# Cross-attention in a decoder kernel: the queries' product ahead of the turn, turned keys beside the turned queries, and two of four masked query copies on ScalarE

## The chip, the core and the metric

The kernel runs on one core of a Trainium2 chip. Its time is device microseconds from the launch's first to its last work; lower is better. TensorE multiplies and transposes into PSUM (eight banks of 128 partitions x 512 f32), VectorE and ScalarE read PSUM and SBUF, GpSimd reads SBUF only. Engines run their instructions in program order and wait for one another on semaphores.

## What is computed

Two decoder layers over 16 samples of 128 tokens with 256 channels. The change lies in the second of six sublayers, the cross-attention of layer 0 (32 heads of 8 channels, queries and keys normalised for each head).

```python
x = x + _L0_attn_ref(_layernorm(x), ...)
x = x + _L0_xattn_ref(_layernorm(x), ctx_2048, L0_xattn_Wq, L0_xattn_Wk, L0_xattn_Wv)   # this one
x = x + _L0_ffn_ref(_layernorm(x), L0_ffn_weight)          # a linear layer with quantised input
x = x + _L1_attn_ref(_layernorm(x), ...)                    # linear attention, then two more
...
def _L0_xattn_ref(x, context, Wq, Wk, Wv):
    q = x @ Wq.T                       # k_raw, v_raw likewise from context, 32 heads of 8
    ...
    q = _rmsnorm(q)                    # over the 8 channels of a head
    k = _rmsnorm(k)
    scores = jnp.einsum('bhnd,bhmd->bhnm', q, k) * scale
    attn = jax.nn.softmax(scores, axis=-1)
    out = jnp.einsum('bhnm,bhmd->bhnd', attn, v)
```

## The kernel before, in words

Each sublayer is a `Part`: on every engine a function `step(s)` issues what is due in step s, for several samples at different stages. In the part "cross-attention and quantised linear" (function `cross_attention_and_quantised_linear`, tensors `xa.*` and `ql.*`) step s handles sample s (its products), b = s-1 (its turn and scores), a = s-2 (weighted values), c = s-3 and d = s-4 (the quantised linear layer), and the layer norms of the samples s+1 and s+2. The steps 6 to 13 are a hardware loop, the others are written out. The order on each engine is the order of the code in `step`; the first steps are interleaved with the last of the channel attention (`ca.*`, through `s.meet()`), the last with the first of the linear attention (`la.*`).

One sample goes through these stages (lines of the kernel before):

- TensorE: the keys' product (L851) and the queries' product (L870), both into PSUM bank 6. ScalarE squares them (L782, `xa.sq`) and copies them to SBUF (L785, tensor `raw` inside `g.spare`). VectorE sums the squares of each head and makes a first guess of the inverse root (L705, L707, L176). GpSimd refines it in ten small instructions (L181 to L199, `xa.norm`).
- VectorE multiplies by it (L685, `xa.qkn`). TensorE transposes the result, "the turn": queries into the first half of bank 5 (`turn2`, L863), keys into bank 4 (`turn`, L865).
- ScalarE copies the turned keys to SBUF (L777, `xa.kT`), VectorE the turned queries four times over, each copy multiplied by another column of the constant `g.quad`, which masks one of four heads in each group of 32 rows (L698, `xa.qT`, 128 x 1024).
- TensorE: scores in two halves of 16 heads (L841 twice) into banks 0 to 3; ScalarE: exponentials of each half (L765). The second half of the scores waits for the exponentials of the first. Weighted values of sample a go to bank 4 (L894), are copied (L797, `xa.oT`), turned into all of bank 5 (L919) and divided (L739, L743); GpSimd adds them to x (L652). The values' product is L924, the turn of the next layer norm L931.
- In between VectorE makes the statistics of the two layer norms (L323 to L327, for `xa.stats` and `ql.stats`), GpSimd their inverse roots (L640, L634), VectorE applies them (L332), and the quantised linear layer takes L721 to L747 on VectorE, L649 on GpSimd, L792 on ScalarE and L881 and L914 on TensorE.

Of the kernel before, what the change touches and what calls it, by code (L numbers as in the profile page):

```python
# [16 lines left out]
ALU = mybir.AluOpType  # L17
ACT = mybir.ActivationFunctionType
AX = mybir.AxisListType

P = 128
# [32 lines left out]
def upto(at, back=0, per=1, more=0):  # L54

    assert at.base is not None or (at.n + 1 - back) * per + more > 0
    return (at.i + (1 - back)) * per + more
# [503 lines left out]
def cross_attention_and_quantised_linear(nc, g, ctx, room):  # L561
# [93 lines left out]
    def vector(dve):  # L655
# [17 lines left out]
        def step(s):  # L673
# [18 lines left out]
            if s.base is None and s.n == 1:  # L692
                s.meet()
            if b.on:
                dve.wait_ge(qk_turned, upto(b))
                if b.past(2):
                    dve.wait_ge(scores_done, upto(b, back=2, per=2))
                nc.vector.tensor_tensor(qT[:, b.par, :, :, :], spread(turn2[:, 0, :, :], 2, 4),  # L698
                                        spread(spread(g.quad[:], 1, C), 3, P), ALU.mult).then_inc(qT_ready, 1)
            if c.on:  # L700
                dve.wait_ge(x_added, upto(c))
                layer_norm_stats(nc, n, g.x[:, c.i, :], c.par, q_var_ready)
            if s.on:
                dve.wait_ge(sq_ready, upto(s))
                nc.vector.tensor_reduce(msq[:, s.par, :], sq[:].rearrange("p (h d) -> p h d", d=HD), AX.X, ALU.add)  # L705
                dve.drain()
                nc.vector.tensor_scalar(msq[:, s.par, :], msq[:, s.par, :], 1.0 / HD, 1e-6, ALU.mult, ALU.add)  # L707
                dve.drain()
                rsqrt_seed(nc, norm[:, s.par, :], msq[:, s.par, :]).then_inc(msq_ready, 1)
# [46 lines left out]
    def scalar(act):  # L756
# [3 lines left out]
        def step(s):  # L760
# [12 lines left out]
            if b.on:  # L773
                act.wait_ge(qk_turned, upto(b))
                if b.past(2):
                    act.wait_ge(scores_done, upto(b, back=2, per=2))
                nc.scalar.activation(kT[:, b.par, :, :], turn[:, 0:D], ACT.Copy).then_inc(kT_ready, 1)  # L777
            if s.on:
# [4 lines left out]
                if s.past(2):  # L783
                    act.wait_ge(qk_ready, upto(s, back=2))
                nc.scalar.activation(raw[:, s.par, :], pqk[:], ACT.Copy).then_inc(raw_ready, 1)  # L785
            if s.base is None and s.n == 0:
                s.meet()
# [29 lines left out]
    def tensor(pe):  # L817
# [9 lines left out]
        def step(s):  # L827
# [24 lines left out]
            if s.base is None and s.n == 1:  # L852
                s.meet()
            if b.on:
                pe.wait_ge(qk_ready, upto(b))
                if b.past(2):
                    pe.wait_ge(o_ready, upto(b, back=2))
                elif not b.past(1):
                    pe.wait_ge(g.ca.vT_ready, B)
                if s.on:  # L860
                    pe.wait_ge(xnT_ready, upto(s))
                for k in range(C):
                    nc.tensor.transpose(turn2[:, 0, k, :], qkn[:, k * P:(k + 1) * P], g.ident[:])  # L863
                for k in range(C):
                    last = nc.tensor.transpose(turn[:, k * P:(k + 1) * P], qkn[:, D + k * P:D + (k + 1) * P], g.ident[:])  # L865
                last.then_inc(qk_turned, 1)
            if s.on:
                pe.wait_ge(xnT_ready, upto(s))
                for k in range(C):
                    last = nc.tensor.matmul(pqk[:, 0:D], xnT[:, s.par, k, :], g.xa_wq[:, k, :], start=(k == 0), stop=(k == C - 1))  # L870
                last.then_inc(qk_done, 1)
            if s.base is None and s.n == 0:
# [10 lines left out]
            if a.on:  # L883
                pe.wait_ge(v_ready, upto(a))
                pe.wait_ge(exp_done, upto(a, per=2))
                if b.on:
                    pe.wait_ge(kT_ready, upto(b))
                if s.on:
# [9 lines left out]
            if b.on:  # L898
                pe.wait_ge(kT_ready, upto(b))
                pe.wait_ge(qT_ready, upto(b))  # L900
# [1696 lines left out]
```

## Time and profile before

| | us |
|---|---|
| Runs: median (lowest to highest of 3) | 1233.75 (1228.12 to 1234.8) |
| The profiled execution, its own time | 1228.39 |
| Its span, first to last instruction | 1226.5 |
| TensorE busy, of the span | 1138.1 (93%) |
| VectorE busy | 781.9 (64%) |
| ScalarE busy | 553.0 (45%) |
| GpSimd busy | 604.8 (49%) |

The part that the change touches has its first work near 100 us and its last near 280 us. The timeline lists instructions in order of time; neighbours of one line are merged ("x4", with the time from the first start to the last end). Bracketed is the time that the engine sat idle before a row, and what ended it. An instruction's duration overlaps the start of the next by some hundredths of a microsecond, so the distance from start to start is what it costs its queue.

### The profile page before, as it was taken

The page shows a single profiled execution, that of the slowest core. Times are in us where ns is not written, and L with a number is a line of the kernel's source. Part 1 is how long each engine was busy: PE and PEld are TensorE (multiplying, and loading weights), DVE is VectorE, ACT ScalarE, POOL GpSimd, SP SyncE. Part 2 cuts the span into 40 slices and gives each one's busy share as a digit, 9 for nine tenths or more (in the row PEclk, how much of TensorE's full clock was granted, in tenths as well). Part 3 has the DMA queues.
Part 4 walks back from the last instruction along what each step waited for, and adds up shares of the span by engine and source line. Part 5 has one row for each costly group of instructions (what it writes and reads, how often), then busy time and mean ns, then how long its engine had stood idle before and what let it go on. Part 6 is the DMA issues. An engine that isn't in the chain of part 4 may idle for free.

```text
span 1226.5 us, 26267 instructions
## 1 busy us (share of the span) xinstructions
PE 1138.1 (93%) x8174; PEld 878.6 (72%) x8175; DVE 781.9 (64%) x1938; ACT 553.0 (45%) x1470; POOL 604.8 (49%) x751
## 2 busy tenths in 40 slices
PE   8998989878999789988999999999997999999996
PEld 5776655544555434467888888888886879999996
DVE  5556788867888769976676767677667644222221
ACT  3444666752333310026666666666665652222221
POOL 2002566644655457755566666666654523323233
PEclk9999999988999989999999999999999999999998
DMA  8000000005999040021000000000001138888884
GB/s 287 0 0 10 14 15 13 13 2 121 189 196 185 2 177 0 4 87 52 6 14 15 14 14 13 17 13 13 17 18 39 62 112 229 243 233 243 237 235 102
DMA packets 57270, 99.87 MB, mean 81 GB/s; under 512 B 5808, under 2 KB 44016, under 8 KB 56432
## 3 DMA queue, kind: packets, MB, share of 16 engines
q1 hardware_dynamic: 42432, 62.92, 20.5%
q10 hardware_dynamic: 7616, 26.74, 6.0%
q0 software_dynamic: 7152, 9.34, 4.3%
q8 instruction: 36, 0.59, 0.2%
q14 instruction: 34, 0.28, 0.1%
HBM read 87.53 MB, written 30.48 MB: 96 GB/s over the span
## 4 chain that ended last, share of the span: by engine, by line
PE 49%; DMA 13%; issue 13%; DVE 9%; ACT 5%; POOL 4%; POOLq 4%; DVEq 2%; ACTq 0%
DMA out<-g.spare,ex.token 13%; PE bank L2230 9%; PE bank L2118 7%; PE bank L2143 4%; PE bank L2127 3%; PE bank L512 2%; PE bank L2194 2%; PE bank L1183 2%; PE bank L1354 2%; PE bank L1355 1%; PE bank L1250 1%; PE bank L2136 1%; ACT ga.e L1986 1%; PE bank L1356 1%; PE bank L1241 1%
## 5 line engine op out<-in xcount | busy, mean ns | idle before, releaser
L2118 PEld LDWEIGHTS bank<-ga.xnT,g.early 128*128 128x128 f32 x1280 | 151.3, 193 | 7.7 <-issue 7.7
L2118 PE MATMUL bank<-ga.xnT,g.early 128*128 128x128 f32 x1280 | 156.4, 276 | 0.0
L1743 POOL TENSOR_TENSOR ga.halves<-ga.halves,g.ga_sinT 128x512 f32<-128x512 f32 x80 | 103.5, 1294 | 62.2 <-ACT ga.halves L1979 62.2
L2230 PE MATMUL bank<-g.early,ga.aT 128*128 128x256 f32 x512 | 117.0, 382 | 0.5 <-ACT ga.aT L2001 0.5
L1986 ACT ACTIVATE ga.e<-bank,ga.negmax 128x128 f32<-128x128 f32 x256 | 90.7, 366 | 48.5 <-DVE ga.negmax L1840 47.6
L1751 POOL TENSOR_TENSOR ga.kqT<-ga.by_cos,ga.halves 128x512 f32<-128x512 f32 x80 | 102.8, 1285 | 16.0 <-issue 16.0
L2230 PEld LDWEIGHTS bank<-g.early,ga.aT 128*128 128x128 f32 x512 | 94.9, 190 | 12.3 <-ACT ga.aT L2001 0.7
L1827 DVE TENSOR_TENSOR ga.by_cos<-bank,g.ga_cosT 128x512 f32<-128x512 f32 x80 | 55.3, 691 | 65.4 <-PE bank L2118 49.0
L2359 DVE TENSOR_TENSOR g.spare<-g.spare,bank 128x512 f32<-128x512 f32 x39 | 26.8, 688 | 97.9 <-PE bank L2416 93.9
L2143 PE MATMUL bank<-ga.pT,ga.v 128*128 128x512 f32 x128 | 68.8, 620 | 12.6 <-ACT ga.pT L1994 12.3
L2407 PEld LDWEIGHTS bank<-g.spare 128*128 128x128 f32 x624 | 75.6, 192 | 1.9
L2416 PE MATMUL bank<-g.spare 128*128 128x128 f32 x624 | 76.2, 275 | 0.0
L2407 PE MATMUL bank<-g.spare 128*128 128x128 f32 x624 | 76.1, 275 | 0.0
L2435 PE MATMUL bank<-g.late,g.spare 128*128 x312 | 74.1, 380 | 0.9 <-DVE g.spare L2365 0.8
L2416 PEld LDWEIGHTS bank<-g.spare 128*128 128x128 f32 x624 | 72.8, 192 | 0.1
L1266 POOL TENSOR_TENSOR g.spare<-g.ctxT 128x1024 f32<-128x1024 f32 x32 | 60.6, 1894 | 20.4 <-PE bank L1356 20.4
L2349 POOL DMA_INDIRECT out<-g.spare,ex.token x39 | 60.9, 1560 | 17.2 <-issue 17.2
L765 ACT ACTIVATE g.late<-bank 128x2048 f32<-128x2048 f32 x32 | 60.1, 1878 | 20.2 <-PE bank L841 20.2
L2345 POOL TENSOR_TENSOR ex.token<-ex.token_d,ga.zero 128x1 uint32<-128x1 uint32 x39 | 7.1, 181 | 118.5 <-DMA out<-g.spare,ex.token 117.5
L2381 ACT ACTIVATE g.spare<-bank 128x512 f32<-128x512 f32 x39 | 23.3, 597 | 92.7 <-PE bank L2407 92.7
L2127 PE MATMUL bank<-ga.kqT 128*128 128x128 f32 x512 | 65.0, 275 | 0.0
L1978 ACT ACTIVATE ga.halves<-bank 64x512 f32<-64x512 f32 x80 | 47.5, 594 | 33.3 <-DVE ga.by_cos L1827 30.9
(310 smaller groups left out, 2610.1 us busy)
## 6 DMA issues: line engine op xcount, KB each, us to landing
g.spare<-in_mo_w SPq DMA_DIRECT2D x39, 512.0 KB, 4.4
g.spare<-in_mo_w ACTq DMA_DIRECT2D x39, 512.0 KB, 4.7
mo_rows<-in_pad_rows SPq DMA_DIRECT2D x1, 18447.0 KB, 106.7
g.spare<-mo_rows SPq DMA_DIRECT2D x39, 129.0 KB, 3.4
g.late<-in_mo_w SPq DMA_DIRECT2D x1, 4096.0 KB, 13.4
g.ctxT<-in_ctxR SPq DMA_DIRECT2D x1, 2048.0 KB, 13.4
xa.ctxT<-in_ctxT SPq DMA_DIRECT2D x16, 128.0 KB, 2.5
g.spare<-cv_rows SPq DMA_DIRECT2D x1, 2048.0 KB, 8.1
```

The source lines that it names most:

```text
L1266: return nc.gpsimd.tensor_tensor(g.cv_kv[:, u % 2, :].rearrange("p (m j i) -> p m j i", j=8, i=8), spread(v, 3, 8), spread(v, 2, 8), ALU.mult)
L1743: nc.gpsimd.tensor_tensor(by_sin[:, par, :].rearrange("p (h t) -> p h t", h=REP), halves[:, par, :].rearrange("p (h t) -> p h t", h=REP), ...
L1751: nc.gpsimd.tensor_tensor(kqT[:, s.par, r, :], by_cos[:, par, :], by_sin[:, par, :], ALU.add).then_inc(kqT_ready, 1)
L1986: last = nc.scalar.activation(e[:, r % 2, j * P:(j + 1) * P], psc[:, r % 2, j * P:(j + 1) * P], ACT.Exp, bias=negmax[:, r % 2, j:j + 1], s ...
L2118: last = nc.tensor.matmul(pkq[:, par, j * P:(j + 1) * P], w[:, q, at * P:(at + 1) * P], xnT[:, s.par, q, :], start=(q == 0), stop=(q == C ...
L2127: last = nc.tensor.matmul(psc[:, r % 2, j * P:(j + 1) * P], kqT[:, b.par, r + 1, j * P:(j + 1) * P], kqT[:, b.par, 0, r * P:(r + 1) * P], ...
L2143: nc.tensor.matmul(paT, v[:, b.par, r * P:(r + 1) * P], pT[:, r % 2, :], start=True, stop=True).then_inc(pv_done, 1)
L2230: last = nc.tensor.matmul(pout, aT[:, h // REP, (h % REP) * P:(h % REP + 1) * P], g.ga_wo[:, h, :], start=(h == 0), stop=(h == H - 1))
L2349: nc.gpsimd.indirect_dma_start(g.acc, bass.IndirectOffsetOnAxis(ap=token[:, b.par, :], axis=0), y[:, b.par, :], None, compute_op=ALU.add). ...
L2407: last = nc.tensor.matmul(p1[:, f * P:(f + 1) * P], w1[:, t.par, c * F + f * P:c * F + (f + 1) * P], xnT[:, t.par, c * P:(c + 1) * P], sta ...
L2416: last = nc.tensor.matmul(p3[:, f * P:(f + 1) * P], w3[:, t.par, c * F + f * P:c * F + (f + 1) * P], xnT[:, t.par, c * P:(c + 1) * P], sta ...
L2435: last = nc.tensor.matmul(py[:, 0:D], hT[:, b.par, f * P:(f + 1) * P], g.mo_w2[:, bass.ds(expert, 1), f, :].rearrange("p e d -> p (e d)"), ...
```

## The change

The turned keys go into the second half of bank 5, beside the turned queries, instead of into bank 4. VectorE writes two of the four masked query copies instead of four, after the keys' copy on ScalarE; ScalarE writes the other two after VectorE's, each with one column of `g.quad` as its scale. On TensorE the queries' product is issued before the turn, no longer behind it. On VectorE the statistics of the linear layer's norm come before the query copies. The weighted values (L894) no longer wait for the keys' copy; the scores wait for ScalarE's query copies as well.

```diff
@@ VectorE
-            if b.on:
-                dve.wait_ge(qk_turned, upto(b))
...
-                nc.vector.tensor_tensor(qT[:, b.par, :, :, :], spread(turn2[:, 0, :, :], 2, 4),
-                                        spread(spread(g.quad[:], 1, C), 3, P), ALU.mult).then_inc(qT_ready, 1)
             if c.on:
                 dve.wait_ge(x_added, upto(c))
                 layer_norm_stats(nc, n, g.x[:, c.i, :], c.par, q_var_ready)
+            if b.on:
+                dve.wait_ge(kT_ready, upto_part(b, 2, 0))
...
+                nc.vector.tensor_tensor(qT[:, b.par, :, 0:2, :], spread(turn2[:, 0, :, :], 2, 2),
+                                        spread(spread(g.quad[:, 0:2], 1, C), 3, P), ALU.mult).then_inc(qT_ready, 1)
@@ ScalarE
-                nc.scalar.activation(kT[:, b.par, :, :], turn[:, 0:D], ACT.Copy).then_inc(kT_ready, 1)
+                nc.scalar.activation(kT[:, b.par, :, :], turn2[:, 1, :, :], ACT.Copy).then_inc(kT_ready, 1)
...
                 nc.scalar.activation(raw[:, s.par, :], pqk[:], ACT.Copy).then_inc(raw_ready, 1)
+            if b.on:
+                act.wait_ge(qT_ready, upto(b))
+                for r in range(2, 4):
+                    last = nc.scalar.activation(qT[:, b.par, :, r, :], turn2[:, 0, :, :], ACT.Copy, scale=g.quad[:, r:r + 1])
+                last.then_inc(kT_ready, 1)
@@ TensorE
+            if s.on:
+                pe.wait_ge(xnT_ready, upto(s))
+                for k in range(C):
+                    last = nc.tensor.matmul(pqk[:, 0:D], xnT[:, s.par, k, :], g.xa_wq[:, k, :], start=(k == 0), stop=(k == C - 1))
+                last.then_inc(qk_done, 1)
             if b.on:
                 pe.wait_ge(qk_ready, upto(b))
...
-                if s.on:
-                    pe.wait_ge(xnT_ready, upto(s))
...
-                    last = nc.tensor.transpose(turn[:, k * P:(k + 1) * P], qkn[:, D + k * P:D + (k + 1) * P], g.ident[:])
+                    last = nc.tensor.transpose(turn2[:, 1, k, :], qkn[:, D + k * P:D + (k + 1) * P], g.ident[:])
                 last.then_inc(qk_turned, 1)
-            if s.on:
-                pe.wait_ge(xnT_ready, upto(s))
-                for k in range(C):
-                    last = nc.tensor.matmul(pqk[:, 0:D], xnT[:, s.par, k, :], g.xa_wq[:, k, :], start=(k == 0), stop=(k == C - 1))
-                last.then_inc(qk_done, 1)
@@
-                if b.on:
-                    pe.wait_ge(kT_ready, upto(b))
...
             if b.on:
-                pe.wait_ge(kT_ready, upto(b))
+                pe.wait_ge(kT_ready, upto(b, per=2))
                 pe.wait_ge(qT_ready, upto(b))
```

TensorE in a step near the middle of the part, before; the names are those of the list above:

```order
L851 MATMUL bank<-g.early,xa.ctxT 128x256 [waits xa.v_ready,xa.raw_ready,xa.ctx_loaded1]
L851 MATMUL bank<-g.early,xa.ctxT 128x256
L863 MATMUL bank<-g.ident,xa.qkn 128x128 [waits xa.xnT_ready,xa.o_ready,xa.qk_ready]
L863 MATMUL bank<-g.ident,xa.qkn 128x128
L865 MATMUL bank<-g.ident,xa.qkn 128x128 x2
L870 MATMUL bank<-g.early,xa.xnT 128x256 [waits xa.xnT_ready]
L870 MATMUL bank<-g.early,xa.xnT 128x256
L881 MATMUL bank<-g.ident_bf,ql.xq 128x128 [waits ql.y_added,ql.xq_ready]
L881 MATMUL bank<-g.ident_bf,ql.xq 128x128
L894 MATMUL bank<-g.late,g.spare 32x128 [waits xa.kT_ready,xa.xnT_ready,xa.exp_done,xa.v_ready]
```

The same step on TensorE after the change:

```order
L856 MATMUL bank<-g.early,xa.ctxT 128x256 [waits xa.v_ready,xa.raw_ready,xa.ctx_loaded1]
L856 MATMUL bank<-g.early,xa.ctxT 128x256
L862 MATMUL bank<-g.early,xa.xnT 128x256 [waits xa.xnT_ready]
L862 MATMUL bank<-g.early,xa.xnT 128x256
L871 MATMUL bank<-g.ident,xa.qkn 128x128 [waits xa.o_ready,xa.qk_ready]
L871 MATMUL bank<-g.ident,xa.qkn 128x128
L873 MATMUL bank<-g.ident,xa.qkn 128x128 x2
L884 MATMUL bank<-g.ident_bf,ql.xq 128x128 [waits ql.y_added,ql.xq_ready]
L884 MATMUL bank<-g.ident_bf,ql.xq 128x128
L895 MATMUL bank<-g.late,g.spare 32x128 [waits xa.xnT_ready,xa.exp_done,xa.v_ready]
```

The queries' product (L870, now L862) has moved ahead of the wait for `qk_ready` (the normalised queries and keys of VectorE's L685); the weighted values have lost a wait.

VectorE in such a step, from the product L685 on, before:

```order
L685 TENSOR_TENSOR xa.qkn<-g.spare,xa.norm 128x512 [waits xa.qk_turned,xa.raw_ready,xa.norm_ready]
L323 BN_STATS xa.stats<-g.x 128x6 [waits xa.xn_ready]
L325 BN_AGGR xa.mv<-xa.stats 128x2
L327 TENSOR_SCALAR xa.mv<-xa.mv 128x1
L698 TENSOR_TENSOR xa.qT<-bank,g.quad 128x1024 [waits xa.scores_done,xa.qk_turned]
L323 BN_STATS ql.stats<-g.x 128x6 [waits xa.x_added]
L325 BN_AGGR ql.mv<-ql.stats 128x2
L327 TENSOR_SCALAR ql.mv<-ql.mv 128x1
L705 TENSOR_REDUCE xa.msq<-xa.sq 128x64 [waits xa.sq_ready]
```

The same piece after the change:

```order
L685 TENSOR_TENSOR xa.qkn<-g.spare,xa.norm 128x512 [waits xa.qk_turned,xa.raw_ready,xa.norm_ready]
L323 BN_STATS xa.stats<-g.x 128x6 [waits xa.xn_ready]
L325 BN_AGGR xa.mv<-xa.stats 128x2
L327 TENSOR_SCALAR xa.mv<-xa.mv 128x1
L323 BN_STATS ql.stats<-g.x 128x6 [waits xa.x_added]
L325 BN_AGGR ql.mv<-ql.stats 128x2
L327 TENSOR_SCALAR ql.mv<-ql.mv 128x1
L701 TENSOR_TENSOR xa.qT<-bank,g.quad 128x2x256 [waits xa.scores_done,xa.kT_ready]
L705 TENSOR_REDUCE xa.msq<-xa.sq 128x64 [waits xa.sq_ready]
```

The query copies stand behind the second set of statistics, are half as large, and wait for ScalarE's copy of the keys.

ScalarE, the same step, after the change:

```order
L777 ACTIVATE xa.kT<-bank 128x256 [waits xa.scores_done,xa.qk_turned]
L782 ACTIVATE xa.sq<-bank 128x512 [waits xa.msq_ready,xa.qk_done]
L785 ACTIVATE g.spare<-bank 128x512 [waits xa.qk_ready]
L789 ACTIVATE xa.qT<-bank,g.quad 128x2x128 [waits xa.qT_ready]
L789 ACTIVATE xa.qT<-bank,g.quad 128x2x128
L797 ACTIVATE ql.xqT<-bank 128x256 [waits ql.xq_turned]
L802 ACTIVATE xa.oT<-bank 128x512 [waits xa.o_turned,xa.pv_done]
L765 ACTIVATE g.late<-bank 128x2048 [waits xa.scores_done,xa.pv_done]
```

The two rows of L789 are new; the rest stands as before (`xa.oT` was L797, `ql.xqT` L792).

## Rows read from the trace of the kernel before

**Rows 1.** The page: busy time of TensorE (part 1), a 512-element VectorE group (part 5).

```profile
PE 1138.1 (93%) x8174; PEld 878.6 (72%) x8175; DVE 781.9 (64%) x1938; ACT 553.0 (45%) x1470; POOL 604.8 (49%) x751
...
L1827 DVE TENSOR_TENSOR ga.by_cos<-bank,g.ga_cosT 128x512 f32<-128x512 f32 x80 | 55.3, 691 | 65.4 <-PE bank L2118 49.0
```

**Rows 2.** Busy time by stretch: start:end, length, engines' busy us, TensorE's granted clock.

```profile
130.00:255.00 125.00, 110.90 (x1370) 73.88 (x1371) 105.05 (x295) 86.64 (x116) 73.61 (x180) 1.00 0.05 13
...
264.00:266.00 2.00, 1.55 (x20) 1.27 (x24) 1.11 (x5) 0.86 (x3) 0.55 (x1) 0.50 0.00 0
```

**Rows 3.** Timeline of VectorE, one step: start, us, line, tensors, [idle before].

```profile
205.91 1.08 DVE L685 TENSOR_TENSOR xa.qkn<-g.spare,xa.norm 128x512 f32<-128x512 f32 x1
206.91 0.41 DVE L323 BATCH_NORM_STATS2 xa.stats<-g.x 128x6 f32 x1
...
207.83 1.22 DVE L698 TENSOR_TENSOR xa.qT<-bank,g.quad 128x1024 f32<-128x1024 f32 x1
208.97 0.42 DVE L323 BATCH_NORM_STATS2 ql.stats<-g.x 128x6 f32 x1
...
209.79 0.68 DVE L705 TENSOR_REDUCE xa.msq<-xa.sq 128x64 f32<-128x512 f32 x1
...
215.56 0.99 DVE L685 TENSOR_TENSOR xa.qkn<-g.spare,xa.norm 128x512 f32<-128x512 f32 x1 [0.53 <-POOL xa.norm L199]
```

**Rows 4.** Timeline of TensorE, the same step.

```profile
205.22 1.13 PE L851 MATMUL bank<-g.early,xa.ctxT 128*128 128x256 f32 x4
207.04 0.44 PE L863 MATMUL bank<-g.ident,xa.qkn 128*128 128x128 f32 x2 [0.69 <-DVE xa.qkn L685]
...
207.54 1.03 PE L870 MATMUL bank<-g.early,xa.xnT 128*128 128x256 f32 x4
208.40 0.28 PE L881 MATMUL bank<-g.ident_bf,ql.xq 128*128 128x128 bf16 x2
...
210.49 1.14 PE L841 MATMUL bank<-xa.qT,xa.kT 32*128 32x512 f32 x8
...
214.70 1.13 PE L851 MATMUL bank<-g.early,xa.ctxT 128*128 128x256 f32 x4
```

**Rows 5.** Timeline of ScalarE, the same step.

```profile
207.74 0.38 ACT L777 ACTIVATE xa.kT<-bank 128x256 f32<-128x256 f32 x1 [0.50 <-PE bank L865]
208.60 0.60 ACT L782 ACTIVATE xa.sq<-bank 128x512 f32<-128x512 f32 x1 [0.48 <-PE bank L870]
```

**Rows 6.** Timeline of GpSimd, the same step.

```profile
206.40 1.18 POOL L652 TENSOR_TENSOR g.x<-g.x,xa.o 128x256 f32 x1
209.96 0.55 POOL L634 TENSOR_TENSOR ql.rstd<-ql.mv,g.minus_half 128x1 f32<-128x1 f32 x1 [2.38 <-DVE ql.mv L327]
```

**Rows 7.** Timeline of VectorE: L685 of samples 3 and 15.

```profile
138.73 1.08 DVE L685 TENSOR_TENSOR xa.qkn<-g.spare,xa.norm 128x512 f32<-128x512 f32 x1 [0.83 <-POOL xa.norm L199]
...
253.64 1.08 DVE L685 TENSOR_TENSOR xa.qkn<-g.spare,xa.norm 128x512 f32<-128x512 f32 x1
```

**Rows 8.** All of line L453: durations ns min/median/max, first and last start.

```profile
L453 ACT ACTIVATE ca.mixed<-bank,ca.rowsum x32: 359/364/368, 17.9 to 111.2; 128x128 f32<-128x128 f32 x32
```

**Rows 9.** Timeline of TensorE, the part's first steps with scores (samples 0, 1).

```profile
112.54 0.38 PE L863 MATMUL bank<-g.ident,xa.qkn 128*128 128x128 f32 x2
...
114.50 1.14 PE L841 MATMUL bank<-xa.qT,xa.kT 32*128 32x512 f32 x8 [0.50 <-issue]
...
119.55 1.13 PE L851 MATMUL bank<-g.early,xa.ctxT 128*128 128x256 f32 x4
121.23 0.44 PE L863 MATMUL bank<-g.ident,xa.qkn 128*128 128x128 f32 x2 [0.56 <-DVE xa.qkn L685]
```

**Rows 10.** Timeline of VectorE: the sum of squares in sample 1's turn step.

```profile
123.42 0.69 DVE L705 TENSOR_REDUCE xa.msq<-xa.sq 128x64 f32<-128x512 f32 x1 [0.27 <-ACT xa.sq L782]
```

**Rows 11.** Timeline of TensorE at the part's end: last first-half scores, next part's turn.

```profile
257.92 1.14 PE L841 MATMUL bank<-xa.qT,xa.kT 32*128 32x512 f32 x8
...
264.45 0.66 PE L1221 MATMUL bank<-g.ident,la.xn 128*128 128x128 f32 x2 [2.20 <-ACT g.late L765]
```

More of the change, by code:

```diff
@@ L693, in step @@
                 s.meet()
-            if b.on:
-                dve.wait_ge(qk_turned, upto(b))
-                if b.past(2):
-                    dve.wait_ge(scores_done, upto(b, back=2, per=2))
-                nc.vector.tensor_tensor(qT[:, b.par, :, :, :], spread(turn2[:, 0, :, :], 2, 4),
-                                        spread(spread(g.quad[:], 1, C), 3, P), ALU.mult).then_inc(qT_ready, 1)
             if c.on:
@@ L702, in step @@
                 layer_norm_stats(nc, n, g.x[:, c.i, :], c.par, q_var_ready)
+            if b.on:
+                dve.wait_ge(kT_ready, upto_part(b, 2, 0))
+                if b.past(2):
+                    dve.wait_ge(scores_done, upto(b, back=2, per=2))
+                nc.vector.tensor_tensor(qT[:, b.par, :, 0:2, :], spread(turn2[:, 0, :, :], 2, 2),
+                                        spread(spread(g.quad[:, 0:2], 1, C), 3, P), ALU.mult).then_inc(qT_ready, 1)
             if s.on:
```

## The prediction

> **What bounds the kernel now.** The page comes first: TensorE is busy 93% of the span, VectorE 64%, GpSimd 49% [rows 1], which invites the reading that only TensorE counts. The busy times by stretch correct that for the part that is changed: from 130 to 255 us, TensorE is busy 110.9 of 125 us and VectorE 105.1, at the full TensorE clock [rows 2]. Neither is quite full, so the order of waits must be read, and the timeline of one step gives it.
>
> Call T the start of VectorE's product L685. VectorE runs without a gap from T = 205.91 to the sum of squares L705 at 209.79, 3.88 us later; the next L685 stands at 215.56, after 0.53 us of idling that GpSimd's `xa.norm` ended [rows 3]. So this ring returns to itself: L685, two sets of statistics, the query copies L698, L705, then 5.77 us of guess, GpSimd's refinement and handing over, and again L685: 3.88 + 5.77 = 9.65 us. From sample 3 to sample 15 the 12 rounds average (253.64 - 138.73) / 12 = 9.58 us [rows 7]. TensorE is the follower: it idles 0.69 us before the turn, until L685 has ended (206.99; the turn starts 0.05 later, which I take as the price of every hand-over) [rows 3, 4]. The ring is VectorE's order plus GpSimd's latency. What leaves it shortens each round.
>
> **The change part by part.**
>
> *VectorE's copies.* L698 costs its queue 207.83 to 208.97 = 1.14 us, 0.08 less than its duration [rows 3]. Half of its 1024 elements remain. The nearest row for 512 elements from PSUM is 691 ns [rows 1], less 0.08 makes 0.61. Gain 1.14 - 0.61 = 0.53 us, inside the ring. As bounds: 0.40 if the doubly repeated form costs a fixed part as large as 0.2 us more, 0.57 if it halves exactly.
>
> *Statistics ahead of the copies.* The same work in another order: 0 on the ring, if its wait is met. It wants x from GpSimd's L652, which ends at 207.58 = T + 1.67 [rows 6]; VectorE arrives at T + 1.92 (207.83). Spare 0.25 us. It makes GpSimd's L634 earlier by more than a microsecond, where that engine idles 2.38 us [rows 6]; no gain, since the refinement behind it waits for L705's sums. VectorE now reaches its copies at T + 1.00 + 0.92 + 0.82 = T + 2.74 (L685, statistics, statistics [rows 3]), which is what hides the new wait below.
>
> *The queries' product ahead of the turn.* Its four passes cost 207.54 to 208.40 = 0.86 us [rows 4]. They now fill TensorE's 0.69 us gap. From L851's start I count 0.96 for it (it lasts 1.13, L870 1.03 at a cost of 0.86 [rows 4]) and 0.86, so the turn can start 1.82 us after L851. Squares of the next sample are ready earlier, but L705 is reached by VectorE only after its copies, so they had been early enough: 0.
>
> *ScalarE's two copies, and the wait in front of them.* New, 256 elements each with a scale from a tile. Such a copy is not in the trace. Low bound: the keys' copy, 256 elements with a fixed scale, 0.38 us [rows 5]. Middle: L453 with its scale from a tile takes 0.364 us for 128 elements [rows 8]; 128 more cost 0.11 (256 more make L782's 0.60 out of L777's 0.38 [rows 5]), together 0.47. High bound: two L453, 0.73. I take 0.47, because it has both the scale and the length, and 0.38 until the second may start: 0.85 for the pair (0.66 to 1.37). ScalarE has room: 86.6 busy of 125 us [rows 2]. Queued behind the wait are the linear layer's copy, the copy of the weighted values and the exponentials.
>
> *The chain through them.* Let U be the start of the turn. Keys' copy starts at U + 0.70 [rows 4, 5], lasts 0.38; hand-over 0.05; VectorE 0.69; 0.05; ScalarE 0.85; 0.05; then the scores. Sum 2.77 us from U, where TensorE's own work (L863, L865 0.50, then 208.40 to 210.49 = 2.09 [rows 4]) needs 2.59. From scores to the next L851 it is 4.21 [rows 4], to the next turn 1.82. So a second ring appears, 2.77 + 4.21 + 1.82 = **8.80 us**. The first ring becomes 9.65 - 0.53 = 9.12, on average 9.58 - 0.53 = **9.05 us**. The longer one governs: VectorE and GpSimd keep the lead, by 0.25 us. In T's terms the scores start at T + 2.74 + 0.69 + 0.05 + 0.85 + 0.05 = T + 4.38 (today T + 4.58), the next turn 6.03 later, T' + 1.36, and its keys' copy is ready at T' + 2.49, before VectorE asks at T' + 2.74. TensorE's old gap reappears before the scores instead of before the turn.
>
> PSUM — Partial Sum Buffer, in the Trainium skill (section "PSUM bank collisions raise a hardware error"), says that two engines may not touch one bank's quadrant at once, reads against reads included. That speaks against this change: with keys and queries in one bank the three readings must go one after the other, as the added waits make them. If they could overlap, the chain from U would shrink and the second ring with it; the first ring, and my sum, would be the same, but the first rival would lose its ground.
>
> *The first steps lose.* There the rings aren't yet running. Sample 0's turn stands at 112.54 with no idle time before it [rows 9]: the product in front makes it 113.40, the scores 113.40 + 2.77 = 116.17 instead of 114.50. L851 follows 5.05 us after the scores (119.55 [rows 9]): 121.22. Sample 1's turn: 123.04 (was 121.23). Its keys are ready 1.13 later, 124.17, VectorE's copies cost 0.61, and L705 is at 124.78 instead of 123.42 [rows 10]: **+1.36 us**. From here the first ring leads; samples 2 to 14 are 13 rounds, 13 x 0.53 = **-6.9**. L685 of sample 15 then stands at 253.64 - 5.5.
>
> *The last step gains.* No product there. The scores of sample 15 came at 257.92, T + 4.28 [rows 7, 11], held up by a full-size L698 behind a late turn; now T + 1.13 + 1.13 + 0.69 + 0.05 + 0.85 + 0.05 = T + 3.90: **-0.4**.
>
> *The rest.* The linear attention starts on these scores' exponentials and is shifted as a whole. No other work in it is changed. Sum: 1.36 - 6.9 - 0.4 = -5.9 us. Of the profiled execution's 1228.4 us this leaves 1222.5. That execution is at the low end of the three runs; I forecast for the median, 1233.75 - 5.9 = 1227.9, or 1228.
>
> **Rivals.**
>
> 1. *The second ring takes over.* It needs 0.25 us more in the chain from U. With ScalarE's copies at their high bound (pair 1.37 instead of 0.85) the ring is 9.32 us, and a round gains 0.26 instead of 0.53: 13 x 0.26 = 3.4, the first steps cost 1.36 + 0.52 and the last 0.52 - 0.4, so about -3.4 + 1.9 + 0.1 = -1.4: 1232. Four hand-overs instead of one speak for it, the row with scale and length against it.
>
> 2. *Slower: the same ring, dearer.* Today's 9.58 us is reached when the chain from U lasts 3.55 instead of 2.77, so when each ScalarE copy costs 0.39 us more than I take. From there every further 0.1 us costs 1.3 us over 13 rounds. With copies of 1.1 us each the chain is 4.03 (0.63 more per copy), the ring 10.06: 13 x 0.48 = 6.2, first steps 1.4 + 1.3, last 1.3 - 0.4: +9.8, 1244. For it: writing two pieces of 128 at a distance from each other. Against it: no row shows such a price for any ScalarE copy.
>
> 3. *TensorE's clock falls in the first steps.* Sample 0's turn ends at about 114.0, its scores come at 116.17: 2.2 us without work. Late in the part 2.20 us of idling stand before L1221, and from 264 to 266 us the granted clock is 0.50, the 1.2 GHz level [rows 2, 11]. The Trainium skill's page TensorE: Matmul & The Clock Gate, section "Part 1: The HAM clock gate (the "warmup" mystery)", has the throttled clock as the default that activity lifts; the trace agrees. L841 of 1.14 us and L851 of 1.13 doubled cost 1 us each, 2 on the way to sample 1's turn: -3.9, so 1230.
>
> 4. *The start costs nothing, or more leaves the ring than L698's half.* Without the 1.36 us and with 0.57 a round: -7.4 - 0.4 = -7.8: 1226.
>
> 5. *No effect.* If x from L652 comes later than assumed, VectorE waits ahead of its copies and gives the 0.53 back; it takes 0.25 to begin and 0.78 to lose all; the first steps' loss and the last one's gain remain, +1.0: 1235.
>
> **How the numbers follow.** Forecast 50% (1226.5 to 1229), rival 1 13%, rival 2 7%, rival 3 11%, rival 4 12%, rival 5 7%. About 0.5%, 6.2 us, is what a measurement of this kernel can tell from no change. The forecast lies just inside it at 5.9, so it is split nearly evenly: 0.24 beyond and 0.26 within. Faster by over 0.5%: 0.24 + rival 4's 0.12 + a little of the others = 0.38. Slower: rival 2, mostly = 0.07. Within: 0.55. The range: the runs before lie 1228.1 to 1234.8, so a median can fall several us under the one shown; with 1228.1 as the base, the forecast gives 1222 and rival 4 1220.5. Above, rivals 1 and 3 are inside, rivals 2 and 5 outside: 1233.5. That is 1220.5 to 1233.5.
>
> **What would show it.** Right: from sample 3 to 15 L685 every 9.0 to 9.1 us; L701 0.69 us and not waiting; ScalarE's new copies 0.47 each; TensorE idle 0.4 to 0.5 us before the first-half scores and hardly before the turn; sample 1's L705 about 1.4 us late; the linear attention as long as before, its start 6 us earlier. Wrong, and how: L701 waiting for the keys' copy means rival 1 or 2; a half clock between 114 and 122 us rival 3; VectorE idle before the `ql` statistics rival 5; a longer part behind 280 us, which the sum holds fixed, would be none of these.

## The result, and the profile after

| | before | after |
|---|---|---|
| Median of 14 runs each, on one chip (us) | 1231.12 | 1225.24 (1222.76 to 1228.56) |
| Ratio, with its 95% interval | | 0.9938 (0.9923 to 0.9952) |
| Again, in a later comparison (after: 6 runs) | 1229.11 | 1225.34; 0.9961 (0.9946 to 0.9976) |
| The profiled execution / its span | 1228.39 / 1226.5 | 1228.56 / 1226.7 |

The change makes the kernel 5.9 us faster by the medians, 7.6 by the ratio; in the later comparison it is 3.8 by the medians. The execution that was profiled after is the slowest of its 14, so the two spans alone would say that nothing happened. The stages must be compared.

The page, busy times after (before: [rows 1]), and the busy times by stretch; the stretch from 130 to 255 us answers to [rows 2], columns as there:

```profile
PE 1141.5 (93%) x8174; PEld 886.4 (72%) x8175; DVE 774.5 (63%) x1938; ACT 562.1 (46%) x1502; POOL 603.1 (49%) x751
```

```profile
130.00:255.00 125.00, 115.26 (x1440) 80.30 (x1442) 102.89 (x304) 98.86 (x149) 77.19 (x191) 0.99 0.05 14
...
119.00:123.00 4.00, 4.00 (x16) 2.34 (x16) 0.62 (x2) 2.52 (x4) 2.27 (x8) 0.57 0.12 35
```

VectorE's total falls by 7.4 us, ScalarE's rises by 9.1. Between 119 and 123 us TensorE's granted clock is 0.57 in the mean, where it was 1.00 before.

Timeline of VectorE, one step after (answers to [rows 3]):

```profile
205.49 1.08 DVE L685 TENSOR_TENSOR xa.qkn<-g.spare,xa.norm 128x512 f32<-128x512 f32 x1
206.50 0.42 DVE L323 BATCH_NORM_STATS2 xa.stats<-g.x 128x6 f32 x1
...
207.40 0.43 DVE L323 BATCH_NORM_STATS2 ql.stats<-g.x 128x6 f32 x1
...
208.35 0.69 DVE L701 TENSOR_TENSOR xa.qT<-bank,g.quad 128x512 f32<-128x512 f32 x1
208.96 0.68 DVE L705 TENSOR_REDUCE xa.msq<-xa.sq 128x64 f32<-128x512 f32 x1
```

Timeline of TensorE, the same step (answers to [rows 4]):

```profile
205.14 1.13 PE L856 MATMUL bank<-g.early,xa.ctxT 128*128 128x256 f32 x4
206.11 1.03 PE L862 MATMUL bank<-g.early,xa.xnT 128*128 128x256 f32 x4
206.97 0.38 PE L871 MATMUL bank<-g.ident,xa.qkn 128*128 128x128 f32 x2
...
207.61 1.95 PE L895 MATMUL bank<-g.late,g.spare 128*32 128x128 f32 x64
209.97 1.14 PE L846 MATMUL bank<-xa.qT,xa.kT 32*128 32x512 f32 x8 [0.40 <-ACT xa.qT L789]
```

Timeline of ScalarE, the same step (answers to [rows 5]):

```profile
207.61 0.38 ACT L777 ACTIVATE xa.kT<-bank 128x256 f32<-128x256 f32 x1 [0.45 <-PE bank L873]
207.89 0.59 ACT L782 ACTIVATE xa.sq<-bank 128x512 f32<-128x512 f32 x1
208.36 0.61 ACT L785 ACTIVATE g.spare<-bank 128x512 f32<-128x512 f32 x1
209.07 0.84 ACT L789 ACTIVATE xa.qT<-bank,g.quad 128x256 f32<-128x256 f32 x2
```

VectorE has no idle time from L685 to L705, and none after it until it waits 0.53 us for GpSimd's `xa.norm` ahead of the next L685, as before. L701 costs its queue 0.61 us, and the ScalarE pair takes 0.84. TensorE doesn't wait before the turn in the middle steps any more; it waits 0.40 us before the scores (0.59 in the step ahead).

In the table, every time is counted from the first sum of squares of the part (L705 at 103.57 us before, at 105.11 after: the trace of after lies 1.54 us later from its first products on, the first of which waits longer for a load of its weights; that is no work of the change). "Round" is the distance of L685 from sample 3 to sample 15, over 12; "turn 0" and "scores 0" are those of sample 0, "squares" is the sum of squares L705 in sample 1's turn step, "handed over" is the first product of the linear attention that reads its turned activations (L1183 before).

| | round | turn 0 | scores 0 | squares | L685(15) | scores 15 | handed over |
|---|---|---|---|---|---|---|---|
| before | 9.576 | 8.97 | 10.93 | 19.85 | 150.07 | 154.35 | 166.94 |
| after | 9.061 | 9.82 | 12.60 | 21.99 | 145.45 | 150.78 | 162.55 |
| split only (e1) | 9.074 | 8.96 | 12.33 | 21.40 | 145.12 | 149.37 | 160.74 |
| product ahead only (e2) | 9.561 | 9.83 | 11.80 | 20.45 | 150.88 | 156.80 | 168.57 |
| statistics behind (e3) | 9.419 | 9.83 | 12.61 | 22.00 | 150.35 | 154.22 | 165.89 |
| product behind (e4) | 9.112 | 8.96 | 12.33 | 21.30 | 145.47 | 149.66 | 161.50 |
| three on ScalarE (e5) | 9.228 | 9.83 | 12.97 | 22.21 | 147.79 | 152.08 | 164.27 |
| eight pieces (e6) | 9.830 | 9.83 | 13.52 | 24.17 | 157.54 | 162.66 | 174.41 |
| first products behind (e7) | 9.059 | 8.95 | 12.32 | 21.34 | 144.78 | 148.97 | 160.76 |
| the change again | 9.075 | 9.83 | 12.61 | 21.99 | 145.65 | 150.96 | 162.50 |
| split, first copies early (e8) | 9.045 | 8.96 | 11.21 | 20.41 | 143.75 | 148.00 | 160.31 |
| norm statistics later (e9) | 9.107 | 10.77 | 13.55 | 22.09 | 145.81 | 149.79 | 161.34 |
| e7, e8's first step, e9 (e10) | 9.106 | 9.91 | 12.58 | 21.74 | 145.56 | 149.54 | 161.12 |

After, the part hands over 4.39 us earlier: +2.14 up to the squares, -6.76 to L685(15), +1.05 to the scores of sample 15, -0.82 behind them (there a stretch at half clock lasts 3.4 us after, 6.8 before). Behind the part the distance between the two traces keeps changing. Counted from TensorE's first matmul, after is 1.3 us late ahead of the part, 3.1 us ahead at the hand-over, 4.3 near 290 us, 2.5 near 450, 5.9 near 530, 4.6 from 570 to 665, 3.4 from 680 on and 1.1 from 950 on. All but one of these jumps stand at stretches of half clock in parts whose code is the same (at 280 us one of 3.4 us, where before has one of 6.8; at 928.1 one of 6.8 and at 941.7 one of 3.4, where before has one of 3.4). The exception, near 670 us, has the full clock: there a cast of two elements on VectorE (L1529) took 1.22 us, where before has 0.17. At TensorE's last matmul 0.7 are left. That is why this one execution shows no gain.

### The profile page after: what moved, and what is told of

It reads as the page before. It is cut to its first block, busy times and chain, and to the rows that moved or that the text cites. A ratio compares the mean times of both kernels' runs of the same rounds, so it can differ in the third digit from the quotient of the medians.

```text
span 1226.7 us, 26308 instructions
## 1 busy us (share of the span) xinstructions
PE 1141.5 (93%) x8174; PEld 886.4 (72%) x8175; DVE 774.5 (63%) x1938; ACT 562.1 (46%) x1502; POOL 603.1 (49%) x751
## 4 chain that ended last, share of the span: by engine, by line
PE 51%; DMA 14%; issue 12%; DVE 8%; ACT 5%; POOLq 4%; POOL 4%; DVEq 2%; ACTq 0%
DMA out<-g.spare,ex.token 13%; PE bank L2231 9%; PE bank L2119 8%; PE bank L2144 4%; PE bank L2128 3%; PE bank L512 2%; PE bank L2195 2%; PE bank L1184 2%; PE bank L1355 2%; PE bank L1356 2%; PE bank L2137 2%; PE bank L1357 2%; PE bank L1251 1%; PE bank L1242 1%; ACT ga.e L1987 1%
## 5 line engine op out<-in xcount | busy, mean ns | idle before, releaser
L2346 POOL TENSOR_TENSOR ex.token<-ex.token_d,ga.zero 128x1 uint32<-128x1 uint32 x39 | 7.0, 180 | 120.1 <-DMA out<-g.spare,ex.token 119.1
```

## The experiments

The theory: VectorE's order, with GpSimd's latency, sets the round; the halved copy alone makes it shorter, statistics ahead of the copies hide the wait for the keys, and the product's new place does nothing there. Its rival: the second ring, from the turn through the copies to the scores, governs or is near. All kernels here compute the whole reference.

### The split alone

Against the kernel before; turned keys stay in bank 4, the product stays behind the turn, the statistics behind the copies, and the weighted values still wait for the keys' copy.

```diff
-                nc.vector.tensor_tensor(qT[:, b.par, :, :, :], spread(turn2[:, 0, :, :], 2, 4), ...
+                nc.vector.tensor_tensor(qT[:, b.par, :, 0:2, :], spread(turn2[:, 0, :, :], 2, 2), ...
@@ ScalarE, behind the raw copy
+                act.wait_ge(qT_ready, upto(b))
+                for r in range(2, 4):
+                    last = nc.scalar.activation(qT[:, b.par, :, r, :], turn2[:, 0, :, :], ACT.Copy, scale=g.quad[:, r:r + 1])
+                last.then_inc(kT_ready, 1)
@@ TensorE, scores
-                pe.wait_ge(kT_ready, upto(b))
+                pe.wait_ge(kT_ready, upto(b, per=2))
```

> Only the split: VectorE writes two query copies, ScalarE the other two, with the keys still turned into bank 4, the product behind the turn and the statistics where they were. The theory is that a ring of VectorE's order and GpSimd's latency sets the round, and that the 0.53 us taken off VectorE is the whole gain: the round from sample 3 to 15 goes from 9.58 to 9.05 us, as in the full change, and the time to 6 to 7 us below the kernel before. The rival, that filling TensorE's gap ahead of the turn (the product moved forward) brings the gain, expects 9.5 us or more here and no gain in time.

Measured: 1225.14 us, 0.9958 of before (0.9940 to 0.9977); round 9.074. Timelines of this kernel, VectorE and then TensorE:

```profile
204.94 1.08 DVE L685 TENSOR_TENSOR xa.qkn<-g.spare,xa.norm 128x512 f32<-128x512 f32 x1
...
206.87 0.69 DVE L698 TENSOR_TENSOR xa.qT<-bank,g.quad 128x512 f32<-128x512 f32 x1
...
216.07 0.69 DVE L698 TENSOR_TENSOR xa.qT<-bank,g.quad 128x512 f32<-128x512 f32 x1 [0.20 <-PE bank L870]
```

```profile
206.08 0.44 PE L868 MATMUL bank<-g.ident,xa.qkn 128*128 128x128 f32 x2 [0.16 <-DVE xa.qkn L685]
...
209.53 1.14 PE L846 MATMUL bank<-xa.qT,xa.kT 32*128 32x512 f32 x8
```

The split alone brings the whole of the shorter round. With the keys in their own bank VectorE never waits for the keys' copy: in the first step shown it waits for nothing, in the next 0.20 us for the turn. Bank sharing is what makes the statistics' new place necessary, and neither is needed for the gain.

### The product ahead of the turn, alone

Against the kernel before, the block of L870 moved in front of the turn's wait, nothing else.

```diff
+            if s.on:
+                pe.wait_ge(xnT_ready, upto(s))
+                for k in range(C): ...      # the queries' product
             if b.on:
                 pe.wait_ge(qk_ready, upto(b))
...
-            if s.on:
-                pe.wait_ge(xnT_ready, upto(s))
-                for k in range(C): ...
```

> Only the queries' product ahead of the turn, all else as in the kernel before. The theory: TensorE follows, so the round stays at 9.5 to 9.6 us, the gap of 0.7 us moves from before the turn to another place, and the first steps lose 0.9 us or more, so the time is the same or up to 2 us more. The rival, TensorE's gap as the cause: round 8.9 to 9.1 us and a gain of 5 us or more.

Measured: 1232.59 us, 1.0024 (1.0002 to 1.0046); round 9.561. By the medians it costs 2.5 us, and the interval just excludes no change. It fills a gap that belonged to a follower, so the round gains 0.015 us, and the turn of sample 0 is 0.86 us later. The hand-over is 1.63 us later; the last step alone loses 1.64 from L685 to the scores, since the weighted values took 3.62 us at half clock there.

### The change with the statistics behind the copies

```diff
@@ VectorE, against the changed kernel
-            if c.on:
-                dve.wait_ge(x_added, upto(c))
-                layer_norm_stats(nc, n, g.x[:, c.i, :], c.par, q_var_ready)
             if b.on:
                 dve.wait_ge(kT_ready, upto_part(b, 2, 0))
...
+            if c.on:
+                dve.wait_ge(x_added, upto(c))
+                layer_norm_stats(nc, n, g.x[:, c.i, :], c.par, q_var_ready)
```

> The full change, but VectorE's statistics of the linear layer's norm stand behind the query copies again. The theory: the keys' copy is ready at T + 2.5, VectorE arrives at T + 1.9 and waits 0.5 to 0.6 us, which eats the gain: round 9.5 to 9.6 us, L698's successor waiting for ScalarE in every step. The rival, that the statistics' place is free because VectorE is not what sets the round: 9.05 us.

Measured: 1228.94 us in its one run (before 1230.08); round 9.419, a little under what was expected. Timeline of VectorE, two steps of this kernel:

```profile
200.93 0.69 DVE L698 TENSOR_TENSOR xa.qT<-bank,g.quad 128x512 f32<-128x512 f32 x1 [0.60 <-ACT xa.kT L777]
...
210.19 0.69 DVE L698 TENSOR_TENSOR xa.qT<-bank,g.quad 128x512 f32<-128x512 f32 x1 [0.34 <-ACT xa.kT L777]
```

The wait for the keys is real, 0.60 and 0.34 us in alternate steps, and stands in VectorE's ring. The statistics' new place is the edit that makes the shared bank harmless: 9.419 - 9.06 = 0.36 us a round.

### The change with the product behind the turn

```diff
@@ TensorE, against the changed kernel: the product block (L862) back behind the turn (L873)
-            if s.on: ...
             if b.on:
                 pe.wait_ge(qk_ready, upto(b))
...
+            if s.on: ...
```

> The full change, but the queries' product stands behind the turn again. The theory: the round stays at 9.05 to 9.1 us, since VectorE and GpSimd set it; the first steps are 1.5 to 2.5 us shorter, so the time is 1 to 2 us below the full change. The rival, TensorE's gap as the cause: the round goes back to 9.5 us and the gain is gone.

Measured: 1225.72 us, 0.9954 (0.9937 to 0.9970); round 9.112, 0.04 to 0.05 dearer than the change, but the hand-over is 1.05 us earlier. The 1 to 2 us below the change that were expected are not seen (0.9954 here, 0.9938 and 0.9961 for the change): inside the change, the product's place is worth nothing that these runs can tell. Alone (e2) it cost time.

### Three copies on ScalarE

```diff
-                nc.vector.tensor_tensor(qT[:, b.par, :, 0:2, :], spread(turn2[:, 0, :, :], 2, 2), ...
+                nc.vector.tensor_tensor(qT[:, b.par, :, 0:1, :], spread(turn2[:, 0, :, :], 2, 1), ...
-                for r in range(2, 4):
+                for r in range(1, 4):
```

> The full change, but VectorE writes one query copy and ScalarE three. By two rings: VectorE and GpSimd lose another 0.27 us (9.05 to 8.78), while the chain from the turn through the copies goes from 2.77 to about 2.88 and its ring from 8.80 to 8.91, which then governs: round 8.9 us. By the first ring alone: 8.78. If the second ring is longer than I count: 9.05 or more.

Measured: round 9.228, a miss; 1230.35 us in its one run (before 1229.11). Timelines of this kernel: VectorE, ScalarE, TensorE.

```profile
199.94 0.42 DVE L701 TENSOR_TENSOR xa.qT<-bank,g.quad 128x256 f32<-128x256 f32 x1 [0.30 <-ACT xa.kT L777]
```

```profile
199.43 0.38 ACT L777 ACTIVATE xa.kT<-bank 128x256 f32<-128x256 f32 x1 [0.53 <-PE bank L873]
199.71 0.59 ACT L782 ACTIVATE xa.sq<-bank 128x512 f32<-128x512 f32 x1
200.19 0.61 ACT L785 ACTIVATE g.spare<-bank 128x512 f32<-128x512 f32 x1
200.67 1.22 ACT L789 ACTIVATE xa.qT<-bank,g.quad 128x256 f32<-128x256 f32 x3
```

```profile
198.72 0.38 PE L871 MATMUL bank<-g.ident,xa.qkn 128*128 128x128 f32 x2
...
201.94 1.14 PE L846 MATMUL bank<-xa.qT,xa.kT 32*128 32x512 f32 x8 [0.62 <-ACT xa.qT L789]
```

The ScalarE copies don't start when VectorE's has ended (199.94 + 0.42 = 200.36), but when ScalarE's own two passes over the products are through its queue: 200.67, which is 1.24 us behind the start of the keys' copy. The prediction followed only the hand-over through VectorE and left ScalarE's order out. From the turn to the scores it is 201.94 - 198.72 = 3.22; with 4.21 and 1.83 behind (the prediction's two distances, the latter 1.83 here) a ring of 9.26, against 9.228 measured (in every other step the 3.22 is 3.14). TensorE doesn't wait before the turn here, so this ring closes. So this kernel runs on the second ring, and rival 1 governs it.

### The second ring made longer on purpose

Each ScalarE copy in four pieces of 64 elements, VectorE as in the change.

```diff
-                    last = nc.scalar.activation(qT[:, b.par, :, r, :], turn2[:, 0, :, :], ACT.Copy, ...)
+                    for c2 in range(C):
+                        for h2 in (slice(0, 64), slice(64, 128)):
+                            last = nc.scalar.activation(qT[:, b.par, c2, r, h2], turn2[:, 0, c2, h2], ACT.Copy, ...)
```

> The full change, but ScalarE writes its two query copies in eight pieces of 64 elements instead of two of 256, which I put at 1.85 instead of 0.85 us (8 x 0.22 from start to start, the last one 0.31). VectorE has the same work. The second ring becomes 8.80 + 1.0 = 9.8 us: round 9.8 us, and VectorE waits for ScalarE's keys' copy in every step. The rival, that only VectorE and GpSimd matter and ScalarE has room, expects 9.05 us.

Measured: round 9.830; 1232.91 us in its one run (before 1229.11). Timelines of this kernel: ScalarE, TensorE, VectorE.

```profile
206.47 1.76 ACT L791 ACTIVATE xa.qT<-bank,g.quad 128x64 f32<-128x64 f32 x8
```

```profile
208.28 1.14 PE L848 MATMUL bank<-xa.qT,xa.kT 32*128 32x512 f32 x8 [1.18 <-ACT xa.qT L791]
```

```profile
205.74 0.69 DVE L701 TENSOR_TENSOR xa.qT<-bank,g.quad 128x512 f32<-128x512 f32 x1 [0.72 <-ACT xa.kT L777]
```

The turn of that step stands at 204.51, so the keys' copy starts at +0.72, the copies 1.24 behind it, and they last 1.76: with 0.05 the chain is 3.77, the ring 3.77 + 4.21 + 1.83 = 9.81, measured 9.83. The second ring's formula holds, once ScalarE's order is in it. VectorE, now the follower, waits 0.72 us for the keys.

### The first steps

Two kernels take the +2.14 us apart. In the first (against the change) the product of steps 1 and 2 stands behind the turn; the change was run beside it once more.

```diff
+            behind = s.base is None and s.n in (1, 2)
+            if s.on and not behind:
+                product()
             if b.on: ...                     # the turn
+            if s.on and behind:
+                product()
```

> The full change, with the product behind the turn in steps 1 and 2 alone, where the products delayed the turn. Expected: scores of sample 0 0.9 us earlier than in the full change, TensorE's clock no longer falling before them (1.4 instead of 2.2 us of idling), L705 of sample 1 some 1.5 to 2 us earlier, the round as it is, 9.06; in time 1 to 2 us below the full change. If the full change's loss in the first steps is made good elsewhere: no difference.

> The full change as it is, to be compared on the same chip: 5.9 to 7.6 us below the kernel before, round 9.06 us, the first scores after 2.2 us of idling; whether TensorE's clock falls there again is open, half of the runs at a guess.

The second is the split alone (e1), with ScalarE's query copies ahead of its squares in step 1.

```diff
+            early = s.base is None and s.n in (1,)
+            if b.on and early:
+                query_copies()
...                                           # squares and raw copy
+            if b.on and not early:
+                query_copies()
```

> The split alone, with one more edit: in step 1 only, ScalarE writes its query copies before it squares and copies the products. In the split alone TensorE waited 1.9 us for the first scores and its clock then stood at 0.5 for 3.4 us. Expected: the first scores 1.1 us earlier (turn + 2.3 instead of 3.4), no half clock between 115 and 122 us, L705 of sample 1 about 1 us earlier, round unchanged at 9.07; time 1 to 1.5 us below the split alone. If the clock falls all the same, or the later squares cost as much as is won: no difference.

Measured: e7 1222.56 us, 0.9954 (0.9941 to 0.9967); the change again 1225.34, 0.9961 (0.9946 to 0.9976); e8 1222.02, 0.9945 (0.9924 to 0.9966). Timelines of the first step with scores: TensorE of the change, of e7 and of e8, then ScalarE of e7.

```profile
114.07 1.03 PE L862 MATMUL bank<-g.early,xa.xnT 128*128 128x256 f32 x4
114.93 0.38 PE L871 MATMUL bank<-g.ident,xa.qkn 128*128 128x128 f32 x2
...
117.71 1.14 PE L846 MATMUL bank<-xa.qT,xa.kT 32*128 32x512 f32 x8 [2.17 <-ACT xa.qT L789]
118.78 1.80 PE L925 MATMUL bank<-g.early,xa.ctxT 128*128 128x256 f32 x4
...
120.93 1.90 PE L846 MATMUL bank<-xa.qT,xa.kT 32*128 32x512 f32 x8
```

```profile
115.90 1.90 PE L846 MATMUL bank<-xa.qT,xa.kT 32*128 32x512 f32 x8 [1.90 <-ACT xa.qT L789]
```

```profile
114.88 1.14 PE L851 MATMUL bank<-xa.qT,xa.kT 32*128 32x512 f32 x8 [0.79 <-ACT xa.qT L781]
```

```profile
113.17 0.38 ACT L777 ACTIVATE xa.kT<-bank 128x256 f32<-128x256 f32 x1 [1.66 <-PE bank L876]
114.04 0.60 ACT L782 ACTIVATE xa.sq<-bank 128x512 f32<-128x512 f32 x1 [0.48 <-PE bank L862]
114.53 0.59 ACT L785 ACTIVATE g.spare<-bank 128x512 f32<-128x512 f32 x1
115.01 0.84 ACT L789 ACTIVATE xa.qT<-bank,g.quad 128x256 f32<-128x256 f32 x2
```

In the change again the clock falls in the same place, after 2.18 us of idling. e7 missed: I had expected the scores 0.9 us earlier and no half clock; they come 0.3 earlier, and the clock falls, since the squares now wait for the product and the query copies queue behind them. e8 shows it: with the copies in front the scores stand at 11.21 instead of 12.33, the squares' sum at 20.41 instead of 21.40, and no stretch of half clock is there. Its hand-over is 2.2 us earlier than the change's, though only 0.4 earlier than e1's: behind its last scores 6.8 us are at half clock, where e1 has 3.4. The medians, 3 us lower, go the same way, but the intervals overlap, so it is not shown that e8 beats the change in the kernel's time.

### Statistics of the next norm out of the ring's front

Against the change: the `xa` statistics behind L705, GpSimd's addition to x first in its order.

```diff
@@ VectorE
-            if n2.on: ...
-                layer_norm_stats(nc, m, g.x[:, n2.i, :], n2.par, var_ready)      # ahead of the ql statistics
...
+            if n2.on: ...                                                         # behind the first guess
+                layer_norm_stats(nc, m, g.x[:, n2.i, :], n2.par, var_ready)
@@ GpSimd: x + xa.o first, then the rounding, then the root for xa
```

> The full change, with the statistics of the next layer norm taken out of the stretch between L685 and L705 (0.92 us) and put behind the guess L176, while GpSimd adds to x before it rounds, and takes the root for those statistics last. The computation is the same. If VectorE's order and GpSimd's latency alone set the round it falls by up to 0.4 us (the linear layer's statistics then wait for x): 8.6 us. If the second ring, through the turn and ScalarE's own queue (2.84 + 4.21 + 1.83 = 8.88 us, now with the squares ahead of the query copies), is what comes next: 8.9 us. VectorE's own work sums to 8.5 and with the wait to 8.9. I expect 8.9; the rival, that nothing below 9.05 is to be had because TensorE sets it: 9.05.

Measured: 1225.10 us, 0.9961 (0.9944 to 0.9978); round 9.107, a miss. Timeline of VectorE of this kernel:

```profile
204.17 1.16 DVE L685 TENSOR_TENSOR xa.qkn<-g.spare,xa.norm 128x512 f32<-128x512 f32 x1
...
206.49 0.69 DVE L697 TENSOR_TENSOR xa.qT<-bank,g.quad 128x512 f32<-128x512 f32 x1 [0.34 <-ACT xa.kT L777]
...
213.07 1.16 DVE L685 TENSOR_TENSOR xa.qkn<-g.spare,xa.norm 128x512 f32<-128x512 f32 x1
```

VectorE no longer waits for GpSimd, and waits for the keys instead, 0.34 us here and 0.59 in the next step; its own work is the rest of the round. With the statistics away from their place nothing covers that wait, as in e3.

The last kernel has e7's edit, e8's first step and e9's order together.

> All that should help together: the full change, the product behind the turn in steps 1 and 2, ScalarE's query copies before the squares in step 1, and the statistics behind L176 as in the run before. Round 8.9 us, first scores about 1 us earlier than with the product behind the turn alone; time 9 to 11 us below the kernel before and 3 to 5 below the full change.

Measured: 1224.43 us, 0.9959 (0.9946 to 0.9972); round 9.106, handed over at 161.12, a miss in all of these. Nothing adds up on top of e7 or e8.

## Why the prediction was right, and where it was not

**The round: right.** Forecast 9.05, measured 9.06. Split by the trace: from L685 to L705 the 12 steps average 3.89 us before and 3.40 after, from L705 to the next L685 5.68 and 5.67. So 0.50 of the 0.53 came where the copy stands, and nothing else moved much: over the 13 rounds -6.9 was forecast, and -6.76 measured. L701's cost of 0.61 was exact; the two sets of statistics cost 0.90 and 0.95 in the step shown, where 0.92 and 0.82 had been taken, 0.11 more. e1 shows the copy as the cause, e2 clears the product, e3 confirms what the statistics hide.

**ScalarE's copies: right, with a hole in the chain.** 0.47 us each (473 ns in the median) and 0.84 for the pair, as estimated from the row with scale and length. The chain left out that they stand behind ScalarE's own squares and raw copy. From the turn it is 0.71 to the keys' copy (0.64 in every other step), 1.24 from there as in e5, 0.84 and 0.05: 2.84, not 2.77 us, and the ring 8.88, not 8.80. In the change this is hidden; it decided e5. The scores came at T + 4.48 instead of T + 4.38, TensorE idle 0.40 before them, as foretold.

**The bank.** With keys and queries in one bank, read one after the other, the round is 9.06; with two banks it is 9.07 (e1), and without the reorder 9.42 (e3). The Trainium skill's page PSUM — Partial Sum Buffer, section "PSUM bank collisions raise a hardware error", forbids the overlap of such readings; no run here tried it. The sum did not hang on it.

**The first steps: +1.36 became +2.14.** The turn of sample 0 (+0.85) and its scores (12.60 against the 12.60 that 116.17 - 103.57 makes) were met. Then the forecast case and rival 3 came together: the scores wait 2.17 us and TensorE's clock is at half for 3.4 us from 119.1 on. L925 took 1.80 instead of 1.13, the second scores 1.90 instead of 1.14, and 0.8 us reached the squares, where the rival had counted 2. The step that failed is to have treated this as another case, with 11%, though its condition, 2.2 us of idling, followed from the forecast's own times.

**The last step: -0.4 became +1.05.** Its reason was wrong. Timeline of TensorE before, around the scores of [rows 11]:

```profile
256.00 1.98 PE L894 MATMUL bank<-g.late,g.spare 128*32 128x128 f32 x64 [0.45 <-ACT xa.kT L777]
257.92 1.14 PE L841 MATMUL bank<-xa.qT,xa.kT 32*128 32x512 f32 x8
```

TensorE has no idle time before those scores: what held them up was L894's wait for the keys, not a full-size L698. The change takes that wait away and puts another in, since this step has no next norm whose statistics would cover it. VectorE and TensorE after:

```profile
252.26 0.43 DVE L323 BATCH_NORM_STATS2 ql.stats<-g.x 128x6 f32<-128x256 f32 x1 [0.62 <-POOL g.x L652]
```

```profile
252.51 3.45 PE L895 MATMUL bank<-g.late,g.spare 128*32 128x128 f32 x64
```

VectorE waits 0.62 us for x: rival 5's mechanism. It does so in the last three steps, none of which has a next norm; in the first two it costs nothing, since VectorE still reaches its copies 2.57 us after L685, where a middle step has 2.86. In the last step the sum had the keys' copy as the last thing waited for, 2.26 us after L685. Without a half clock the 2.57 leave 4.19 us from L685 to the scores (e4, e7), -0.1 against before's 4.28. In the profiled execution the weighted values also fell into half clock, 3.45 us instead of 1.96.

**The rest: not fixed.** The sum held the time behind the part fixed. Between the two traces the distance goes from 3.1 us at the hand-over up to 5.9 and down to 0.7 there, at stretches of half clock and, for 1.2 us of it, at one long instruction of VectorE. Executions of one kernel differ by as much as the change brings: one of the change took 1220.12 us at a mean clock of 0.985, the five others of that comparison 1224.4 to 1226.5 at 0.980 to 0.982.

**The number.** Forecast 1228, -5.9 on the median shown; measured 1225.24, -5.9 on the median of the same comparison. The base moved, by 2.6 us; that the difference agrees to the tenth is partly luck. In the trace the three terms of the sum make 2.14 - 6.76 + 1.05 = -3.6 us instead of -5.9, and 0.8 more came behind the last scores, where the stretch at half clock is shorter and the sum had nothing. The interval of the first comparison reaches from 5.9 to 9.5 us, and the later one gives 3.8 by the medians.

## What to carry to other kernels

Find the ring by following one engine's order from an instruction back to itself, and shorten what lies on it: half of one copy gave everything here, while filling the idle time of the engine that follows gave nothing. When an operation is appended to an engine's queue, its start is the later of its releaser and its own queue; count both. The first and last steps lack some of the work that covers waits in the middle, so walk through them row by row with the new order.

## What the runs showed of the hardware

A long wait of TensorE is no sure sign of a half clock. Before the first scores TensorE idled 1.90 to 3.09 us in nine of the profiled executions. In eight of them, the change (2.17) and e7 (1.90) among them, the clock then stood at the 1.2 GHz level for 3.4 us or more; in e9, with 2.18 us, it did not. In the four with 0.50 to 1.36 us, e8 (0.79) among them, it did not fall there either. The rows of e9:

```profile
116.66 1.14 PE L846 MATMUL bank<-xa.qT,xa.kT 32*128 32x512 f32 x8 [2.18 <-ACT xa.qT L789]
117.73 1.13 PE L925 MATMUL bank<-g.early,xa.ctxT 128*128 128x256 f32 x4
```

In the last step it fell after a wait of 1.42 and 1.44 us before the turn (the change, twice) and of 1.91 (e2), not after 1.41 (e7), 1.70 (before) or 2.18 (e3). What tells these cases apart stays open. Nor was it tried to keep TensorE busy in these waits.

VectorE's L685 and GpSimd's operations on 256 elements lengthen one another, and it is the one that starts second that gets long. L685 takes 0.69 us with none of them beside it (samples 0 and 1 before). In the change the rounding starts 0.08 us ahead of L685 and keeps its 0.61; L685 takes 1.08, and the addition to x, which starts while L685 runs, takes 1.18, where it has 0.73 in the last steps. In e9 the addition comes first and keeps 0.73, and the rounding, started while L685 runs, takes 1.07. Timelines of GpSimd, the change and e9 (the change's L685 is shown above, at 205.49):

```profile
205.41 0.61 POOL L649 TENSOR_TENSOR ql.xq<-ql.rounded,ql.magic 128x256 bf16<-128x256 f32 x1
205.98 1.18 POOL L652 TENSOR_TENSOR g.x<-g.x,xa.o 128x256 f32 x1
```

```profile
212.96 0.73 POOL L641 TENSOR_TENSOR g.x<-g.x,xa.o 128x256 f32 x1 [0.23 <-DVE xa.o L743]
213.64 1.07 POOL L646 TENSOR_TENSOR ql.xq<-ql.rounded,ql.magic 128x256 bf16<-128x256 f32 x1
```

In one step of e9 L685 comes first, and then it keeps its 0.69 us and the addition pays. Timelines of VectorE and of GpSimd:

```profile
139.64 0.69 DVE L685 TENSOR_TENSOR xa.qkn<-g.spare,xa.norm 128x512 f32<-128x512 f32 x1
```

```profile
139.73 1.19 POOL L641 TENSOR_TENSOR g.x<-g.x,xa.o 128x256 f32<-128x256 f32 x1
```

Reordering GpSimd in e9 therefore moved the price rather than removing it: L685 itself takes 1.16 us there. A kernel in which neither starts beside L685 was not tried.
